# Three moves in the schedule of a two-layer graph network kernel: squares a step later, fp16 parts ahead of one-hots, key products ahead of key sums

## The chip, the cores and the metric

The kernel runs on one core of a Trainium2 chip. The metric is the device time of one execution in microseconds (us). Before the change three runs gave a median of 366.03 us (365.54 to 366.22).

## The reference

The input is `x` (1250 rows of 512 features) and 20000 edges `src -> dst`. Two layers follow one another, each on the row-normalized and rectified input:

```python
h = jnp.maximum(_layernorm(x), 0.0)
# layer 0: mean over the neighbours of the batch-normalized rows, a convolution, and attention
xn   = _batchnorm(h, norm1_g, norm1_b)
agg  = segment_sum(xn[src], dst) / maximum(deg, 1)
conv = relu(agg @ W_conv + b_conv)
qf, kf = phi(q, True), phi(k, False)            # 8 heads, exp(u - diag - max)/16 + 1e-6
kv   = einsum('bhnm,bhnd->bhmd', kf, vm)        # the key sums
attn = einsum('bhnm,bhmd->bhnd', qf, kv) * z
x = x + _batchnorm(conv + (attn @ Wo)[batch, pos] + h, norm2_g, norm2_b)
# layer 1
h = jnp.maximum(_layernorm(x), 0.0)
z = (1 + eps) * h + segment_sum(h[src], dst)
h = relu(batch_norm(relu(batch_norm(z @ W1 + b1)) @ W2 + b2))
x = x + h
```

Attention runs over 256 positions of one graph (the last of them stands for all later rows), with 8 heads of 64 and 256 random features (`proj`).

## The kernel before

The edges are never gathered. The kernel first builds the matrix `AT` of edge counts: 25 windows of 50 destinations each. For a window t, VectorE builds `S` (the one-hot lanes of the sources, `first_lanes`, L1139, one instruction of L984) and `ring` (one-hot codes, eight instructions of L988 in `first_chunks`, L1145). TensorE multiplies them into a bank (the counting of step t, eight products of 125x125 by up to 500 columns), and ScalarE copies the bank into `AT` (L779). VectorE builds the one-hots of window t+1 in its step t. The lanes of t+1 wait until the counting of t-1 is done (L1142). Behind them come the low counts of t-1 (L1236, a branch that here only gives a signal), on which later counting into the same bank waits (L1705); from step 8 all counting goes into bank 0, so the counting of step t waits for the low-counts signal of step t-1, which VectorE gives in its step t.

The rest of layer 0 is spread by hand over the 25 steps in the table `SLOTS` (L76), one entry per step and a last one. TensorE runs the pieces of its entry in their order and then the counting of the step (L1696 to L1729). ScalarE runs in each step (L753 to L793) the copies of its pieces, then the copy of `AT`, then normalization of further rows, and at the end the pieces UQ and MX. VectorE runs (L1231 to L1263) lanes, low counts, one-hots, statistics of transposed rows, and then its pieces. The pieces are:

- hT0 to hT9: transposes of the ten row tiles into `hT`. hT7 and hT9 use the same bank, so hT9 waits for ScalarE's copy of hT7.
- K, Q, V, N, PT, P: projections, norms of the heads, transposed `proj`, layout of the norms (`diag`).
- UKg and UQg, g = 0 to 3: products of the keys or queries of two heads with `proj` (the key products of a pair). UK banks 2 and 3 are released by ScalarE once the exponentials of MXg have read them.
- MXg: VectorE's row maximum `kmax` of UKg goes over TensorE to all partitions, VectorE makes `nbk` of it, and ScalarE computes `kf` with four exponentials (L636, L637) and two scalings (L642).
- KVg: TensorE sums kf times values (the key sums of a pair). It waits for both scalings of its pair.
- UQg: VectorE's `qmax` and `nbq`, ScalarE's `qf`; QTg: transposes of qf; Og: attention output.
- G0 to G9: the convolution product of row tile i. ScalarE normalizes the tile into `hn` (`normed`, L677; tile 1 in step 7, tile i+2 behind the AT copy of the step that has Gi), VectorE splits it into two fp16 parts (`normed_parts`, L1097: `hn_hi` L1102, `hn_lo` L1103), and TensorE multiplies the parts with the fp16 parts of the weights in twelve products of 128x512 columns. Tile 0 is multiplied in fp32. In VectorE's step t the parts of tile t-7 are made, t = 8 to 16. ScalarE copies the result to `hh` and VectorE makes the rest `hl` (`conv_low`, L1170), which frees the bank.
- FR: the sum of the squares of the convolution weights. ScalarE squares the weights in step `SQ_AT` (L773), TensorE sums over partitions in piece FR, GpSimd takes the inverse root (`wscale`, L513), ScalarE makes `wC_hi` behind the AT copy of the step that has FR (L780), and VectorE makes `wC_lo` in step `SPLIT_AT` = 6.
- D, A: degrees, and the aggregation over neighbours, twenty products of 400 or 450 columns each; F1, F2, TA, WO: scales of the next weights, and the output projection.

Behind step 24 the rest of the aggregation runs, then the second layer's normalization, aggregation, and two large matrix products. All engines run in the order of their program; waits are semaphores.

Of the kernel before, what the change touches and what calls it, by code (L numbers as in the profile page):

```python
# [15 lines left out]
P = 128  # L16
# [9 lines left out]
T = 10  # L26
# [34 lines left out]
for _n, _k in PARAMS:  # L61
# [12 lines left out]


SLOTS = [s.split() for s in (  # L76
# [4 lines left out]
SQ_AT, SPLIT_AT, H_AT = 2, 6, 6  # L81

SPARE = {"start": 20, "ranges": 5, "hT0": 3, "hT1": 3, "hT2": 4}

# [116 lines left out]
def gnn_kernel(nc, x, src, dst, params, eps, w_conv, wq, wk, wv, wo, proj, w1, w2, out):  # L201
    with ExitStack() as ctx:
        sems = {}

        def sem(name):
            if name not in sems:
                sems[name] = ctx.enter_context(nc.semaphore(name))
            return sems[name]
# [708 lines left out]
        def _(dve):  # L917
# [18 lines left out]
            def row_stats(i):  # L936
                dve.wait_ge(sem(f"d_x{i // 2}"), 32)
                own.step(dve.bn_stats(st_row[:, i % 2, :], x_tile(i)))  # L938
                own.step(dve.bn_aggr(mv_row[:, i, :], st_row[:, i % 2, :]))  # L939
                row_terms(i).then_inc(sem("s_mv"), 1)  # L940
# [40 lines left out]
            def lanes(slot, c):  # L981

                a = slo[:, bass.ds(c, G)].unsqueeze(1).broadcast_to([CH, P, G])
                dve.tensor_tensor(S[:, slot], iota_lane[0:CH], a, ALU.is_equal)  # L984

            def one_hot(slot, t, c, j, a, b):

                return dve.tensor_scalar(ring[:, slot, j, a:b], iota_code[0:CH, a:b], code[:, bass.ds(c + j, 1)],  # L988
                                         float(-CODES * t), ALU.subtract, ALU.is_equal)
# [70 lines left out]
            def weight_low(layer, half):  # L1060
                dve.wait_ge(sem(f"s_w{layer + 1}h"), half + 1)
                lo, hi, raw_w = ((w1_lo, w1_hi, w1_s), (w2_lo, w2_hi, w2_s))[layer]
                k = raw_w[half].shape[1]
                ks = slice(k * half, k * half + k)
                dve.scalar_tensor_tensor(lo[:, ks, :], raw_w[half][:], scale_w[layer][:, 0:1], hi[:, ks, :],
                                         ALU.mult, ALU.subtract).then_inc(sem(f"s_w{layer + 1}l"), 1)
# [25 lines left out]
            def tile_stats(i):  # L1092
                dve.wait_ge(free[PLACE[f"hT{i}"][0]], PLACE[f"hT{i}"][1] + 1)
                for f in range(FB):
                    own.mark(dve.bn_stats(st_1[:, f, i, :], hT[:, f, i * L:(i + 1) * L]))  # L1095

            def normed_parts(i):  # L1097

                dve.wait_ge(sem("s_hn"), i + 1)
                if i >= 3:  # L1100
                    dve.wait_ge(full[PLACE[f"G{i - 2}"][0]], PLACE[f"G{i - 2}"][1] + 1)
                own.step(dve.tensor_copy(hn_hi[:, i % 2], hn[:, i % 2]))  # L1102
                dve.tensor_tensor(hn_lo[:, i % 2], hn[:, i % 2], hn_hi[:, i % 2], ALU.subtract).then_inc(sem("s_hns"), 1)  # L1103
# [4 lines left out]
            def feature_terms(f, n):  # L1108
                return dve.tensor_scalar(var_eps[:, f:f + n], mv_f[:, f:f + n, 1], BN_EPS, None, ALU.add)  # L1109
# [14 lines left out]
            def low_counts(t):  # L1124

                if t == 0:
                    dve.wait_ge(sem("s_atlo0"), 1)
                with dve.If_lt(big_r, span_r):
                    dve.wait_ge(sem("s_at"), t + 1)
                    dve.tensor_tensor(at_of(ATlo, t), counts_of(t), at_of(AT, t), ALU.subtract, saturate=False)\  # L1130
                       .then_inc(sem(f"s_lo{t % 2}"), 1)
                with dve.Else():
                    dve.wait_ge(sem("s_win"), t + 1)
                    dve.sem_inc(sem(f"s_lo{t % 2}"), 1)

            def load_range(t):
                dve.load([lo_r[t % 2], out_r[t % 2]], win[t:t + 1, :])  # L1137

            def first_lanes(t):  # L1139

                if t >= 2:
                    dve.wait_ge(sem("s_win"), t - 1)  # L1142
                lanes(t % 2, dve.snap(lo_r[t % 2], min_val=0, max_val=NCH - 1))

            def first_chunks(t):  # L1145

                lo = dve.snap(lo_r[t % 2], min_val=0, max_val=NCH - 1)
                for n, j in enumerate(CHUNK_ORDER):
                    ins = one_hot(t % 2, t, lo, j, *CHUNK_COLS[j])
                    if n % Q == Q - 1:  # L1150
                        ins.then_inc(sem("s_hot"), 1)
                dve.reg_add(made, made, 1)

            def further_chunks(t):

                dve.reg_add(span_r, out_r[t % 2], 0)
                with dve.If_lt(none_r, span_r):
                    for h in range(2):
                        dve.load([from_r, to_r], ranges[2 * t + h:2 * t + h + 1, :])
                        with dve.Fori(dve.snap(from_r, min_val=0, max_val=NCH - 1),  # L1160
                                      dve.snap(to_r, min_val=1, max_val=NCH), G) as i:
                            dve.wait_ge(sem("s_grp"), dve.snap(made, min_val=1, max_val=1 << 20))
                            lanes(t % 2, i)
                            for j in range(G):
                                ins = one_hot(t % 2, t, i, j, h * HALF, (h + 1) * HALF)
                            ins.then_inc(sem("s_hotx"), 1)
                            dve.reg_add(made, made, 1)
                dve.end_ifs()
# [37 lines left out]
            def piece(name):  # L1206
                if name[0] == "A":
                    mean_rows(name)
                elif name[0] == "G":
                    conv_low(int(name[1]))  # L1210
                else:
                    attention(name)
                if name == "WO1":
                    att_in[0] = True
                    own.after(own.n)
                    for early in RAW:
                        f, ci = int(early[1]), int(early[2])
                        if early in held:
                            own.mark(feature_stats(f, ci, hT[:, f, COLS[ci][0]:sum(COLS[ci])]))
# [11 lines left out]
            for t in range(NW):  # L1231

                if t + 1 < NW:
                    first_lanes(t + 1)
                if t:
                    low_counts(t - 1)  # L1236
                further_chunks(t)
                if t + 1 < NW:
                    first_chunks(t + 1)
                if t + 2 < NW:  # L1240
                    load_range(t + 2)
                if t == 0:
                    for i in range(6, T):
                        row_stats(i)
                for name in SLOTS[t - 1] if t else ():
                    if name[:2] == "hT":
                        tile_stats(int(name[2]))
                        if name == f"hT{T - 1}":
                            own.after(own.n)
                            for f in range(FB):  # L1250
                                own.mark(dve.bn_aggr(mv_f[:, f, :], st_1[:, f].rearrange("p c s -> p (c s)")))
                            own.after(own.n)
                            feature_terms(0, FB).then_inc(sem("s_mv1"), 1)
                if t == SPLIT_AT:
                    dve.wait_ge(sem("s_wch"), 1)
                    dve.scalar_tensor_tensor(wC_lo[:], wC[:], wscale[:, 0:1], wC_hi[:], ALU.mult, ALU.subtract)\
                       .then_inc(sem("s_wcl"), 1)
                if 0 < t - H_AT - 1 < T:
                    normed_parts(t - H_AT - 1)
                for name in SLOTS[t]:  # L1260
                    piece(name)
                    if name == "O3":
                        weight_low(0, 0)  # L1263
# [612 lines left out]
```

## Time and profile before

| | |
|---|---|
| median of 3 runs | 366.03 us (365.54 to 366.22) |
| the profiled execution | 365.55 us |
| its span from first to last instruction | 363.7 us |
| TensorE busy | 348.0 us, 96% |
| VectorE busy | 246.4 us, 68% |
| ScalarE busy | 181.3 us, 50% |
| GpSimd busy | 95.2 us, 26% |
| mean granted clock of TensorE | 0.998 |

The span is the time between the first and the last instruction in the trace; the execution's time has some 1.85 us around it. All times in the rows below count from the start of the span. Busy time of TensorE is modelled: its products overlap. Steps 0 to 7 take up to about 59 us, steps 8 to 24 up to about 160 us.

### The profile page before, as it was taken

To read this page: it belongs to the slowest core of one execution; us is meant where nothing else is said; L and a number is where in the kernel's file an instruction comes from. 1 tells how busy PE (TensorE), PEld (TensorE's weight loads), DVE (VectorE), ACT (ScalarE), POOL (GpSimd) and SP (SyncE) were. 2 spreads that over 40 slices of the span, in tenths; PEclk is the share of its full clock that TensorE was granted. 3 is DMA by queue.
4 is the path that set the end of the run, shared out by engine and by line. 5 is a ranking of instruction groups with operands and counts; after the bars stand their busy time and mean duration, and the time that the engine had idled before them with its cause. 6 is when DMAs were issued, how large, how long until landed. Compare 5 with 4: busy or idle time off the path is not lost.

```text
span 363.7 us, 6194 instructions
## 1 busy us (share of the span) xinstructions
PE 348.0 (96%) x2072; PEld 224.0 (62%) x2072; DVE 246.4 (68%) x667; ACT 181.3 (50%) x302; POOL 95.2 (26%) x163
## 2 busy tenths in 40 slices
PE   7899899989999999999998999999999999999994
PEld 3678655757777666767564675455555555565562
DVE  5889999998998995867998787522464443422325
ACT  0548538768477167454437766411534645233132
POOL 8132120000000000100042778722277465101100
PEclk9999999999999999999999999999999999999999
DMA  6990303300000000034900000000000000010223
GB/s 162 289 303 30 119 1 119 118 3 1 3 3 4 3 3 3 3 97 148 264 9 3 0 2 3 2 2 1 2 0 0 2 0 2 0 51 21 70 58 85
DMA packets 13539, 18.05 MB, mean 50 GB/s; under 512 B 1839, under 2 KB 6895, under 8 KB 13491
## 3 DMA queue, kind: packets, MB, share of 16 engines
q1 hardware_dynamic: 12538, 17.21, 16.4%
q8 instruction: 26, 0.43, 0.5%
q10 hardware_dynamic: 953, 0.23, 0.3%
q14 instruction: 22, 0.18, 0.2%
HBM read 14.88 MB, written 2.56 MB: 48 GB/s over the span
## 4 chain that ended last, share of the span: by engine, by line
PE 74%; DVE 15%; issue 4%; ACT 3%; DVEq 2%; DMA 0%; POOL 0%; SPq 0%; ACTq 0%; POOLq 0%
PE bank L1424 71%; DVE ring L988 2%; DVE st L1095 2%; DVE st_row L938 2%; PE bank L1815 1%; PE bank L1454 1%; PE bank L1774 1%; ACT hn L688 1%; DVEq L1137 1%; DVE st_row L1310 1%; DVE x L1305 1%; DVE mv_row L939 1%; DVE x L1375 0%; PE bank L1635 0%; DVE ln_tmp L933 0%
## 5 line engine op out<-in xcount | busy, mean ns | idle before, releaser
L1424 PE MATMUL bank<-AT,hh 125*128 125x400 f16 (+3 forms) x250 | 81.2, 332 | 1.2 <-DVEq L1335 0.4
L1424 PE MATMUL bank<-AT,hl 125*128 125x400 f16 (+3 forms) x250 | 80.9, 332 | 0.0
L988 DVE TENSOR_SCALAR ring<-iota_code,code 125x250 f16<-125x250 f16 x200 | 46.1, 307 | 1.4 <-issue 1.4
L1424 PEld LDWEIGHTS bank<-AT,hh 125*128 125x128 f16 x250 | 24.1, 97 | 19.8 <-issue 1.1
L1424 PEld LDWEIGHTS bank<-AT,hl 125*128 125x128 f16 x250 | 24.2, 97 | 17.6 <-issue 0.2
L1424 PE MATMUL bank<-ring,S 125*128 125x250 f16 x200 | 33.5, 310 | 0.0
L1424 PE MATMUL bank<-a_hi,w_hi 128*128 128x400 f16 (+1 forms) x96 | 32.6, 340 | 0.0
L1424 PE MATMUL bank<-agg_hi,w_hi 128*128 128x400 f16 (+1 forms) x96 | 32.6, 339 | 0.0
L1424 PE MATMUL bank<-agg_hi,w_lo 128*128 128x400 f16 (+1 forms) x96 | 32.5, 339 | 0.0
L1424 PE MATMUL bank<-a_hi,w_lo 128*128 128x400 f16 (+1 forms) x96 | 32.5, 339 | 0.0
L1424 PE MATMUL bank<-agg_lo,w_hi 128*128 128x400 f16 (+1 forms) x96 | 32.5, 339 | 0.0
L1424 PE MATMUL bank<-a_lo,w_hi 128*128 128x400 f16 (+1 forms) x96 | 32.5, 338 | 0.0
L525 POOL TENSOR_SCALAR mean_w<-mean_w 128x1 f32<-128x1 f32 x2 | 0.9, 447 | 119.8 <-ACT mean_w L591 119.8
L1424 PEld LDWEIGHTS bank<-ring,S 125*128 125x128 f16 x200 | 25.7, 145 | 9.1 <-issue 1.4
L861 ACT ACTIVATE zr<-bank,par,undo_w 128x400 f32<-128x400 f32 (+1 forms) x24 | 16.0, 690 | 23.5 <-POOL a_lo L565 17.1
L565 POOL TENSOR_TENSOR a_lo<-zr,a_hi 128x1250 f16<-128x1250 f32 x7 | 22.0, 3141 | 16.7 <-DVE a_hi L1346 16.7
L1090 DVE BATCH_NORM_STATS2 st_f<-zr 128x6 f32<-128x400 f32 (+1 forms) x24 | 13.5, 588 | 18.1 <-ACT zr L861 18.1
L885 ACT ACTIVATE ur<-bank,par,undo_w 128x400 f32<-128x400 f32 (+1 forms) x12 | 8.2, 698 | 32.7 <-PE bank L1424 22.2
L500 POOL TENSOR_TENSOR bn_tmp<-var_eps,minus_half 128x1 f32<-128x1 f32 (+1 forms) x15 | 8.7, 580 | 54.5 <-DVE var_eps L1109 54.5
L591 ACT ACTIVATE AT<-bank 125x500 f16<-125x500 f32 x25 | 15.2, 606 | 12.0 <-PE bank L1424 11.9
L491 POOL TENSOR_TENSOR ln_s<-ln_tmp,minus_half 125x1 f32<-125x1 f32 x20 | 14.5, 723 | 24.3 <-DVE ln_tmp L934 24.3
L984 DVE TENSOR_TENSOR S<-iota_lane,slo 125x1024 f16<-125x1024 f16 x25 | 18.5, 742 | 2.5 <-issue 1.9
(229 smaller groups left out, 703.0 us busy)
## 6 DMA issues: line engine op xcount, KB each, us to landing
w_s<-w SPq DMA_DIRECT2D x4, 1024.0 KB, 5.2
x_in<-x SPq DMA_DIRECT2D x5, 448.0 KB
x<-x SPq DMA_DIRECT2D x2, 1120.0 KB
out<-x SPq DMA_DIRECT2D x6, 224.0 KB
wB<-wk SPq DMA_DIRECT2D x1, 1024.0 KB, 9.6
wA<-wq SPq DMA_DIRECT2D x1, 1024.0 KB, 13.8
wC<-w_conv SPq DMA_DIRECT2D x1, 1024.0 KB, 16.1
wB<-wv SPq DMA_DIRECT2D x1, 1024.0 KB, 6.3
```

The lines of the kernel that those rows point to most:

```text
L491: own.step(pool.tensor_tensor(s, ln_tmp[:, 0, i:i + n], minus_half[0:L, 0:n], ALU.pow))
L500: own.step(pool.tensor_tensor(bn_tmp[:, 1, k:k + n], var_eps[:, k:k + n], minus_half[:, 0:n], ALU.pow))
L565: pool.tensor_tensor(a_lo[:, b, :], zr[:, b % 2, :], a_hi[:, b, :], ALU.subtract)\
L591: return act.activation(o, i, ACT.Copy, scale=scale)
L861: ins = act.activation(zr[:, b % 2, c0:c0 + w], ps[:, 0:w], ACT.Identity, bias=pcol("b1", b), scale=undo_w[0][:, 0:1])
L885: ins = act.activation(ur[:, f % 2, c0:c0 + w], ps[:, 0:w], ACT.Identity, bias=pcol("b2", f), scale=undo_w[1][:, 0:1])
L938: own.step(dve.bn_stats(st_row[:, i % 2, :], x_tile(i)))
L984: dve.tensor_tensor(S[:, slot], iota_lane[0:CH], a, ALU.is_equal)
L988: return dve.tensor_scalar(ring[:, slot, j, a:b], iota_code[0:CH, a:b], code[:, bass.ds(c + j, 1)], float(-CODES * t), ALU.subtract, ALU.i ...
L1090: return dve.bn_stats(st_f[:, f, ci, :], ap)
L1095: own.mark(dve.bn_stats(st_1[:, f, i, :], hT[:, f, i * L:(i + 1) * L]))
L1424: return pe.matmul(o, l, r, start=start, stop=stop, skip_group_check=True)
```

## The change

It makes three moves. ScalarE squares the convolution weights in step 3 instead of 2 (`SQ_AT`), and FR moves from slot 4 to slot 5; with it ScalarE's `wC_hi` moves behind the AT copy of step 5. VectorE makes the fp16 parts of a row tile between the lanes and the one-hots of its step instead of behind the one-hots. In slot 13 UK2 comes before KV1 on TensorE. VectorE's and ScalarE's own order in slot 13 stays, as VectorE has no work for KV1 and ScalarE none for UK2. No instruction is added or taken away, and no DMA is moved.

```diff
-    "hT0 hT1 hT2 K0 RG K1", "hT3 hT4 PT Q0", "hT5 hT6 N1 Q1", "hT7 hT8 N0 hT9 UK0", "FR P", "UQ0 V0", "MX0 V1", "QT0",
-    "G0 UK1", "KV0 UQ1 G1", "O0 G2", "G3 MX1", "QT1 G4", "KV1 UK2 G5", "O1 UQ2 G6", "G7",
+    "hT0 hT1 hT2 K0 RG K1", "hT3 hT4 PT Q0", "hT5 hT6 N1 Q1", "hT7 hT8 N0 hT9 UK0", "P", "FR UQ0 V0", "MX0 V1", "QT0",
+    "G0 UK1", "KV0 UQ1 G1", "O0 G2", "G3 MX1", "QT1 G4", "UK2 KV1 G5", "O1 UQ2 G6", "G7",
...
-SQ_AT, SPLIT_AT, H_AT = 2, 6, 6
+SQ_AT, SPLIT_AT, H_AT = 3, 6, 6
...
                 further_chunks(t)
+                if 0 < t - H_AT - 1 < T:
+                    normed_parts(t - H_AT - 1)
                 if t + 1 < NW:
                     first_chunks(t + 1)
...
-                if 0 < t - H_AT - 1 < T:
-                    normed_parts(t - H_AT - 1)
                 for name in SLOTS[t]:
                     piece(name)
```

## Rows read from the trace of the kernel before

**Rows 1.** Busy time by stretch: start:end, length, engines, clock, DMA share, GB/s
```profile
88.39:189.00 100.61, 100.61 (x633) 70.55 (x634) 84.42 (x206) 53.08 (x91) 5.40 (x13) 1.00 0.17 49
...
90.42:111.40 20.98, 20.98 (x127) 15.28 (x128) 19.84 (x61) 12.41 (x29) 0.00 (x0) 1.00 0.01 2
```

**Rows 2.** TensorE's waits up to 200 us: line <- releaser: us, times, longest
```profile
PE bank L1424 <- issue: 1.6, 1, 1.6
PE bank L1454 <- ACT hT L591: 1.5, 1, 1.5
...
PE bank L1424 <- ACT kf L642: 0.4, 1, 0.4
```

**Rows 3.** The chain of waits, 40 to 100 us: start, us, what
```profile
53.48 0.70 DVE qmax L1019
...
59.07 18.25 PE bank L1424 x104
```

**Rows 4.** VectorE's waits, 29 to 60 us
```profile
DVE ring L988 <- issue: 0.6, 2, 0.4
```

**Rows 5.** ScalarE in order of time: start, us, instruction, [idle before <- releaser]
```profile
36.65 1.91 ACT L694 ACTIVATE sqr<-wC 128x2048 f32<-128x2048 f32 x1
...
54.76 0.47 ACT L653 ACTIVATE qf<-bank,nbq 128x256 f32<-128x256 f32 x1 [2.97 <-DVE nbq L1020]
...
64.44 1.65 ACT L688 ACTIVATE hn<-hT,bn_t,bn_s 128x125 f32<-128x125 f32 x4
...
85.37 0.46 ACT L636 ACTIVATE kf<-bank,nbk 128x256 f32<-128x256 f32 x1
...
90.12 1.65 ACT L688 ACTIVATE hn<-hT,bn_t,bn_s 128x125 f32<-128x125 f32 x4
...
111.44 0.47 ACT L636 ACTIVATE kf<-bank,nbk 128x256 f32<-128x256 f32 x1 [0.65 <-DVE nbk L1013]
```

**Rows 6.** VectorE in order of time, steps 8, 9, 10, 11, 12 and 15
```profile
64.12 1.84 DVE L988 TENSOR_SCALAR ring<-iota_code,code 125x250 f16<-125x250 f16 x8
66.13 0.42 DVE L1102 CAST hn_hi<-hn 128x500 f16<-128x500 f32 x1 [0.17 <-ACT hn L688]
...
69.32 0.83 DVE L984 TENSOR_TENSOR S<-iota_lane,slo 125x1024 f16<-125x1024 f16 x1 [0.26 <-DVE kmax L1004]
...
75.34 0.68 DVE L984 TENSOR_TENSOR S<-iota_lane,slo 125x1024 f16<-125x1024 f16 x1
75.94 1.84 DVE L988 TENSOR_SCALAR ring<-iota_code,code 125x250 f16<-125x250 f16 x8
77.69 0.42 DVE L1102 CAST hn_hi<-hn 128x500 f16<-128x500 f32 x1
78.14 0.68 DVE L1103 TENSOR_TENSOR hn_lo<-hn,hn_hi 128x500 f16<-128x500 f32 x1
...
84.71 0.17 DVE L1013 SCALAR_TENSOR_TENSOR nbk<-diag,kmaxall 128x4 f32<-128x4 f32 x1
...
89.81 0.69 DVE L1172 TENSOR_TENSOR hl<-bank,hh 125x512 f16<-125x512 f32 x1 [1.04 <-ACT hh L591]
...
106.67 0.69 DVE L1172 TENSOR_TENSOR hl<-bank,hh 125x512 f16<-125x512 f32 x1 [0.56 <-ACT hh L591]
```

**Rows 7.** TensorE in order of time: counting 9, G3, KV1, UK2, KV2
```profile
70.50 1.33 PE L1424 MATMUL bank<-ring,S 125*128 125x250 f16 x8
...
78.92 0.40 PE L1424 MATMUL bank<-wC_hi,hn_hi 128*125 128x512 f16 x1 [1.60 <-issue]
...
88.39 1.97 PE L1424 MATMUL bank<-vaug,kf 128*128 128x65 f32 x16 [0.43 <-ACT kf L642]
90.29 1.14 PE L1424 MATMUL bank<-projT,tqk 64*128 64x256 f32 x8
...
114.64 1.90 PE L1424 MATMUL bank<-vaug,kf 128*128 128x65 f32 x16
```

## The prediction

> **What bounds the kernel.** I read the table of stretches first. From 88.39 to 189 us TensorE is busy for 100.61 of 100.61 us [rows 1]: whatever moves the product that starts at 88.39 moves the end by as much, unless a new wait opens in that stretch. Then I read TensorE's own waits [rows 2]. Up to 88.39 three of them answer to the three edits: 1.5 us for a bank that ScalarE's copy of `hT` frees (at 38 us), 1.6 us ahead of 78.92 and 0.4 us ahead of 88.39. The chain of waits says which of them count [rows 3]: it goes through VectorE's qmax at 53.48, two steps of ScalarE, and TensorE from 59.07 on. So up to 59 us VectorE sets the pace, and what it waits for there is its own issue, 0.6 us in all, never another engine [rows 4]. From 59 us TensorE sets it, with VectorE close behind.
>
> **Edit 1: the squares of the convolution weights in step 3 instead of 2, FR in slot 5, wC_hi after the counts of step 5.** ScalarE's squares (about 2 us from 36.65 [rows 5]) no longer stand ahead of the copies of hT7, hT8 and N0, which then run at about 37.3 to 38.6, so hT9 on TensorE loses its wait of 1.5 us. The squares run at about 39 to 41, ahead of AT(3), whose reader is the counting of step 5. wC_hi (2 us, like the squares of the same 128x2048) lands near 50.3, where ScalarE idles 2.97 us up to 54.76 for the first nbq [rows 5]; VectorE's wC_lo wants it after 57. As VectorE waits for nobody before 59, TensorE only arrives earlier at the transposes QT0 and waits 1.5 us longer there; G0 still starts at 59.07. No DMA moves, SP's and ACT's DMA queues keep their order, and POOL's wscale comes before the batch scales as it did. Value taken: 0. Ends: -1.5 us (the whole wait of TensorE) and +0.5 us (a late wC_hi pushes the first qf).
>
> **Edit 2: the fp16 parts ahead of the next one-hots.** In step t VectorE now runs lanes(t+1), parts(t-7), eight one-hots(t+1), pieces. This first bites in step 8 with parts(1). Before, the one-hots ran from 64.12 and the parts began at 66.13 after a rest of 0.17 us of waiting for `hn` [rows 6]. That `hn` is ScalarE's work of 64.44 + 1.65 [rows 5], and nothing in the diff makes it earlier: it stands behind kf of MX0 and qfT of QT0. So VectorE now stands still from about 64.1 to 66.13, and the one-hots that filled this time come behind the parts. Queued behind the waiting instruction are the one-hots (75.94 to 77.69 in a set without a gap, so 1.76 us [rows 6]), hl(0) and kmax. All of VectorE from there on comes 1.76 us later: lanes(10) at 69.32 + 1.76 = 71.08.
> Two instructions of TensorE feel it. The counting of step 9 waits for the low-counts signal that VectorE gives right behind lanes(10); I put this at 0.3 us behind (it lies between 0 and the 0.7 us to the first one-hot): 71.4 instead of 70.50 [rows 7], 0.9 us of new idle. The other is G3, at 78.92. Its parts(3) stood behind lanes(11) at 75.34 and the one-hots at 75.94, and ended at 78.14 + 0.68 = 78.82 [rows 6]. Now lanes(11) start at 75.34 + 1.76 = 77.10, parts(3) 0.60 us later, and they end 1.13 us on (77.69 to 78.82), at 78.83. The lead given to the parts is eaten by the slip that the wait in step 8 made, and G3 starts at 78.93; the 0.9 us at step 9 vanishes in front of this. Value at G3: 0, with ends of -1.6 us (no slip arrives) and +0.3 us (0.1 us more of issue in each of three steps).
>
> **Edit 3 with the slip, steps 11 to 13.** VectorE works without a wait for others from lanes(11) to MX1's nbk, which ended at 84.71 + 0.17 = 84.88 and now ends at 86.64 [rows 6]. ScalarE's kf of MX1 started at 85.37 behind hn(5); it is now bound by nbk (0.04 us behind it) and starts at 86.68, 1.3 us later. KV1 waited for it and began at 88.39, 3.02 us behind the first instruction of kf [rows 5, 7]; KV1 can now begin at 86.68 + 3.02 = 89.7. In the old order UK2 would be stuck behind. Now UK2 (90.29 to 91.35 before, 1.06 us) goes first: its two banks are released when the fourth exponential of MX1 is done, near 88.3, so it runs from about 88.4 to 89.5, inside the wait. KV1 takes 1.90 us (88.39 to 90.29 [rows 7]), and G5 begins at 91.59 against 91.35: +0.24 us. The swap is worth its 1.06 us: without it this would be +1.3.
>
> **Further on: KV2.** Behind kf, ScalarE makes qfT(1), hh(4) and hn(6), all 1.3 us later. VectorE waited for hh(4) already, 1.04 us ahead of 89.81 [rows 6], and its lanes(14), first in a stretch that starts at 90.42, now start at 91.72. Parts(6) then have to wait for hn(6), 90.12 + 1.65 + 1.3 = 93.07 [rows 5], some 0.6 us behind the lanes. From lanes(14) to the nbk of MX2 VectorE took 20.98 us (90.42 to 111.40, 19.84 busy [rows 1]); 0.56 us of it was a wait for hh(7) [rows 6] that is covered when VectorE is late, and I take off 0.1 for smaller ones: 20.3 us. New nbk: 91.72 + 0.6 + 20.3 = 112.62, 1.22 us later. kf began at 111.44 right behind nbk, so KV2 was possible at 111.44 + 3.02 = 114.46 and started at 114.64: a margin of 0.18 us [rows 5, 7]. KV2 moves to 114.46 + 1.22 = 115.68: +1.04 us. Ends: +1.6 us (the whole slip of 1.76 less 0.18) and -0.6 us (VectorE at its 19.84 busy and no new wait). In slot 18 KV2 still stands ahead of UK3, so nothing fills this wait. After it TensorE was busy without a gap, so the shift stays.
>
> **Sum.** These are positions on one engine, one behind the other, and aren't added: 0 for edit 1, 0 at G3, +0.24 at G5, +1.04 at KV2 and at the end. The profiled execution took 365.55 us (span 363.7 and 1.85 around it), which gives 366.6; the median of the runs shown is 0.48 above that execution, so the median comes to 366.03 + 1.04 = 367.1.
>
> **A rule that speaks against this.** TensorE, the busiest engine, has gaps of 1.6 and 0.4 us on the chain and one of 1.5 off it, and the three edits meet them one by one. The Trainium skill (Perfetto Trace Analysis, Optimization Strategy) says to find the gaps of the engine that one optimizes and to make the dependencies behind them start sooner or end faster. By that rule the time falls by 2.0 us, to 364.0. That these gaps end with VectorE's parts and ScalarE's kf the trace confirms; what the rule leaves out is what the earlier start takes from the engine behind.
>
> **Rivals.**
> A, faster: the gaps close. It is one mechanism, the wait for hn(1) in step 8. If it costs VectorE less than about 0.9 us, or lanes(11) have made up for it, parts(3) end before 78.0 and G3 starts up to 1.5 us sooner. Then kf of MX1 starts at 84.92 behind the old nbk (0.45 us sooner), KV1 at 87.94 behind UK2, and G5 at 89.84: -1.5 us. From lanes(14) on VectorE's 20.3 us stand in front of KV2 again and let through 0.5 to 0.7 us of this. So 365.4, or 364.5 if they don't. For it: all three of [rows 2]. Against: an `hn` that ends at 66.1 with VectorE there at 64.1.
> B, no change that can be told: the slip arrives, but VectorE regains more than I let it (the difference between 20.3 and 19.84, and hn(6) sooner), and KV2 comes 0.2 to 0.6 us late: 366.4. For it: the margins here are tenths. Against: nothing idles on VectorE in most steps.
> C, slower by more: in each step the parts now wait for an `hn` that ScalarE makes only after the counting that also releases VectorE's lanes. If ScalarE is late with it in steps 14 to 16 too, or issue gaps of 0.2 us come in several steps, the shift at KV2 is the full 1.6 us and the counting of step 15 waits too: 367.8.
>
> **Chances and range.** My forecast 0.42, C 0.10, B 0.33, A 0.15. 0.2% (0.73 us) is about what a measurement of this kernel can tell from no change: faster by more 0.15, within it 0.33, slower by more 0.52. The range goes from A's capped case, 365.4, to just over C, 367.9; the forecast's own is 366.8 to 367.5.
>
> **What would show it.** VectorE idle for about 2 us at 64 with `hn` as releaser and its one-hots from 67.2; new idle of TensorE up to 71.4; G3 at 78.9; no wait ahead of hT9, a longer one ahead of QT0, G0 at 59.07; UK2 at 88.4 ahead of KV1 at 89.7; a wait of about 0.8 us for kf ahead of KV2. The prediction is wrong if G3 starts before 78.3 or KV2 starts without a wait.

## The result

The changed kernel takes 367.11 us (median of 8 runs, 366.97 to 367.42) against 366.02 us before (8 runs, 365.54 to 366.22): ratio 1.0029, 95% interval 1.0020 to 1.0039. It is 1.1 us slower. The profiled execution took 367.12 us, its span is 365.3 us.

TensorE's waits up to 200 us in the trace after (line <- releaser: us in total, times, longest), to be held against [rows 2]:

```profile
PE bank L1424 <- DVEq L1134: 1.7, 2, 1.2
...
PE bank L1424 <- DVE diag L999: 1.5, 1, 1.5
...
PE bank L1424 <- ACT kf L642: 0.8, 1, 0.8
PE bank L1635 <- ACT qf L654: 0.6, 1, 0.6
```

The wait for ScalarE's copy of `hT` at 38 us is gone, and so is the one of 1.6 us ahead of G3. In their place stand two waits for the low-counts signal of VectorE's sequencer (L1134, 1.7 us), one for a bank that VectorE's `diag` copy frees (1.5 us), and the wait for kf, which has grown from 0.4 to 0.8 us and moved from KV1 to KV2.

VectorE in the trace after, steps 8 to 13 and 16 (start, us, instruction, [idle before <- releaser]), to be held against [rows 6]:

```profile
63.41 0.82 DVE L984 TENSOR_TENSOR S<-iota_lane,slo 125x1024 f16<-125x1024 f16 x1
66.16 0.42 DVE L1102 CAST hn_hi<-hn 128x500 f16<-128x500 f32 x1 [1.92 <-ACT hn L688]
66.61 0.68 DVE L1103 TENSOR_TENSOR hn_lo<-hn,hn_hi 128x500 f16<-128x500 f32 x1
67.21 1.84 DVE L988 TENSOR_SCALAR ring<-iota_code,code 125x250 f16<-125x250 f16 x8
...
71.10 0.83 DVE L984 TENSOR_TENSOR S<-iota_lane,slo 125x1024 f16<-125x1024 f16 x1 [0.26 <-DVE kmax L1004]
...
77.63 0.41 DVE L1102 CAST hn_hi<-hn 128x500 f16<-128x500 f32 x1
78.07 0.68 DVE L1103 TENSOR_TENSOR hn_lo<-hn,hn_hi 128x500 f16<-128x500 f32 x1
...
86.40 0.16 DVE L1013 SCALAR_TENSOR_TENSOR nbk<-diag,kmaxall 128x4 f32<-128x4 f32 x1 [0.15 <-DVE kmaxall L1010]
...
91.06 0.69 DVE L1172 TENSOR_TENSOR hl<-bank,hh 125x512 f16<-125x512 f32 x1 [0.62 <-ACT hh L591]
...
93.06 0.42 DVE L1102 CAST hn_hi<-hn 128x500 f16<-128x500 f32 x1 [0.57 <-ACT hn L688]
...
112.39 0.16 DVE L1013 SCALAR_TENSOR_TENSOR nbk<-diag,kmaxall 128x4 f32<-128x4 f32 x1 [0.15 <-DVE kmaxall L1010]
```

The first pair of rows is where it begins: the lanes at 63.41, then 1.92 us of nothing until `hn` of tile 1 is there, and only then the parts and the one-hots. From then on VectorE is 1.7 to 1.8 us late (lanes(10) at 71.10 instead of 69.32), and it carries this to the nbk of MX1 (86.40 instead of 84.71); at the nbk of MX2 1.15 us are left (112.39 for 111.24).

ScalarE in the trace after, kf of MX1 and of MX2, to be held against [rows 5]:

```profile
86.59 0.47 ACT L636 ACTIVATE kf<-bank,nbk 128x256 f32<-128x256 f32 x1 [1.12 <-DVE nbk L1013]
...
112.58 0.47 ACT L636 ACTIVATE kf<-bank,nbk 128x256 f32<-128x256 f32 x1 [1.74 <-DVE nbk L1013]
```

TensorE in the trace after: MX0, the counting of step 9, G3, the counting of step 12, UK2, KV1, KV2, to be held against [rows 7]:

```profile
50.81 0.68 PE L1424 MATMUL bank<-ident,kmax 128*128 128x128 f32 x4 [1.45 <-DVE diag L999]
...
71.87 1.36 PE L1424 MATMUL bank<-ring,S 125*128 125x250 f16 x8 [1.18 <-DVEq L1134]
...
78.85 0.40 PE L1424 MATMUL bank<-wC_hi,hn_hi 128*125 128x512 f16 x1
...
87.31 1.36 PE L1424 MATMUL bank<-ring,S 125*128 125x250 f16 x8 [0.53 <-DVEq L1134]
88.60 1.13 PE L1424 MATMUL bank<-projT,tqk 64*128 64x256 f32 x8
89.66 2.00 PE L1424 MATMUL bank<-vaug,kf 128*128 128x65 f32 x16
...
115.63 1.97 PE L1424 MATMUL bank<-vaug,kf 128*128 128x65 f32 x16 [0.78 <-ACT kf L642]
```

G3 starts 0.07 us sooner than before, KV2 0.99 us later. As a landmark late in layer 0 I take VectorE picking up the last unit but one of the aggregation, before and after:

```profile
188.97 0.47 DVE L1192 TENSOR_TENSOR tmpr<-bank,rdb 128x300 f32<-128x300 f32 x1
```
```profile
190.03 0.47 DVE L1192 TENSOR_TENSOR tmpr<-bank,rdb 128x300 f32<-128x300 f32 x1
```

It is 1.06 us late. That agrees with the 1.09 us between the medians. The two profiled spans differ by 1.6 us, more than this. Most of the rest is one row of the chain of waits, the same instruction of GpSimd on the same data, before and after:

```profile
222.15 0.55 POOL ln_s L491
```
```profile
223.21 0.93 POOL ln_s L491
```

It took 0.38 us longer in the profiled execution after, in a place where everything waits for it. The last section shows that this step of 0.38 us comes and goes from execution to execution, in kernels of either order, so it isn't put down to the change.

### The profile page after: what moved, and what is told of

It reads as the page before. It is cut to its first block, busy times and chain, and to the rows that moved or that the text cites. A ratio compares the mean times of both kernels' runs of the same rounds, so it can differ in the third digit from the quotient of the medians.

```text
span 365.3 us, 6194 instructions
## 1 busy us (share of the span) xinstructions
PE 349.0 (96%) x2072; PEld 223.7 (61%) x2072; DVE 245.9 (67%) x667; ACT 181.6 (50%) x302; POOL 95.0 (26%) x163
## 4 chain that ended last, share of the span: by engine, by line
PE 61%; DVE 23%; issue 6%; ACT 4%; DVEq 4%; DMA 1%; POOL 0%; SPq 0%; ACTq 0%; POOLq 0%
PE bank L1424 58%; DVE ring L988 5%; DVEq L1137 2%; DVE st L1095 2%; DVE st_row L938 2%; DVE qmax L1019 1%; DVEq L988 1%; DVE kmax L1004 1%; PE bank L1815 1%; DVE hn_hi L1102 1%; PE bank L1454 1%; PE bank L1774 1%; ACT hn L688 1%; DVE S L984 1%; ACT kf L637 1%
## 5 line engine op out<-in xcount | busy, mean ns | idle before, releaser
L491 POOL TENSOR_TENSOR ln_s<-ln_tmp,minus_half 125x1 f32<-125x1 f32 x20 | 14.3, 716 | 24.8 <-DVE ln_tmp L934 24.8
```

What stands on the lines that cost most here:

```text
L491: own.step(pool.tensor_tensor(s, ln_tmp[:, 0, i:i + n], minus_half[0:L, 0:n], ALU.pow))
```

## The experiments

My theory: edit 1 is worth nothing; edit 2 makes VectorE wait for hn(1) in step 8, and this lateness takes back what the parts gained at G3 and then delays kf of MX2; edit 3 hides part of the delay at KV1. The rivals R1 to R8 stand in the expectations. Each run is compared with the kernel before on the same chip (medians 365.60 to 366.08 us).

**Edit 1 alone (e1).**

```diff
-    ... "FR P", "UQ0 V0", ...
+    ... "P", "FR UQ0 V0", ...
-SQ_AT, SPLIT_AT, H_AT = 2, 6, 6
+SQ_AT, SPLIT_AT, H_AT = 3, 6, 6
```

> Only edit 1 (squares in step 3, FR in slot 5) in the kernel before. My theory (VectorE sets the pace up to 59 us, so this edit is worth nothing; all of the loss is the wait for hn(1) that edit 2 makes in step 8): no wait ahead of hT9, about 1.5 us of new TensorE idle between 49 and 57 us, G0 at 59.1, time as before, 366.0 (+-0.2). Rival R1 (a gap that is closed on TensorE is a gain): 1.5 us less, 364.5.

Measured: 366.07 us, ratio 1.0003 (0.9994 to 1.0012). TensorE's waits show where the 1.5 us went:

```profile
PE bank L1424 <- issue: 1.6, 1, 1.6
PE bank L1424 <- DVE diag L999: 1.5, 1, 1.5
```

The wait for `hT` is gone and one of equal length for VectorE's `diag` has taken its place; that ahead of G3 is untouched. G0 stands at 59.43 for 59.07, but VectorE's first lanes, at 15.14 for 14.78, show the same 0.36 us long before the edit acts. R1 falls.

**Edit 2 alone (e2).**

```diff
                 further_chunks(t)
+                if 0 < t - H_AT - 1 < T:
+                    normed_parts(t - H_AT - 1)
...
-                if 0 < t - H_AT - 1 < T:
-                    normed_parts(t - H_AT - 1)
```

> Only edit 2 (the parts ahead of the one-hots in steps 8 to 16). My theory: VectorE idle 1.9 us ahead of parts(1), G3 at 78.9, kf of MX1 at 86.6, KV1 at 89.7 with UK2 behind it, G5 at 92.6 instead of 91.35; KV2 is reached at 115.9 and finds its kf ready (115.6), so its wait is gone: +1.27 us, 367.3. Rival R2 (the order UK2 before KV1 is what costs): as before, 366.0.

Measured: 367.99 us, ratio 1.0054 (1.0040 to 1.0068): 2.0 us slower, where I expected 1.27. R2 falls, as the loss is there without edit 3, and greater. The profile is of a longer execution (372.21 us; the other five took 367.95 to 368.05), in which TensorE's rows stand 4.31 us later already at G0 (63.38 for 59.07): KV1 at 93.89 is 89.58 on the other traces' scale. KV1, UK2 and KV2 in it:

```profile
93.89 1.97 PE L1424 MATMUL bank<-vaug,kf 128*128 128x65 f32 x16 [0.96 <-ACT kf L642]
95.79 1.13 PE L1424 MATMUL bank<-projT,tqk 64*128 64x256 f32 x8
...
120.79 1.97 PE L1424 MATMUL bank<-vaug,kf 128*128 128x65 f32 x16 [0.64 <-ACT kf L642]
```

KV1 waits 0.96 us with UK2 behind it, as expected, but KV2 waits as well, 0.64 us. VectorE says why, in steps 15 and 16:

```profile
109.72 0.42 DVE L1102 CAST hn_hi<-hn 128x500 f16<-128x500 f32 x1 [0.23 <-ACT hn L688]
...
114.18 0.42 DVE L1102 CAST hn_hi<-hn 128x500 f16<-128x500 f32 x1 [0.37 <-ACT hn L688]
```

Once TensorE is 1.2 us late (KV1 at 89.58 for 88.39), ScalarE's `hn`, made behind the counting, is late for VectorE too, and each such wait is handed on to the next nbk. This is the mechanism of my rival C. KV2, at 120.79, is 1.84 us late by the same scale, and the landmark, at 195.19, 1.91 us. So edit 3 is worth 0.85 us beside edit 2 (367.99 here to 367.14 in e10 below), not the 0.2 us that I had left for it.

**Edit 3 alone (e3).**

```diff
-    ... "KV1 UK2 G5", ...
+    ... "UK2 KV1 G5", ...
```

> Only edit 3 (UK2 ahead of KV1). My theory: UK2 runs 88.0 to 89.0 in the wait of KV1, KV1 at 89.0 without a wait, G5 0.43 us sooner, and since hh(7) and the lanes follow TensorE there, KV2 also 0.43 us sooner: 365.6. Rival R2 (the swap itself costs): 366.3 or more.

Measured: 365.92 us, ratio 0.9998 (0.9989 to 1.0007): no change, where I expected 0.43 us less. KV1 and G8 in its trace:

```profile
88.94 2.00 PE L1424 MATMUL bank<-vaug,kf 128*128 128x65 f32 x16
...
106.09 0.40 PE L1424 MATMUL bank<-wC_hi,hn_hi 128*125 128x512 f16 x1 [0.48 <-issue]
```

KV1 no longer waits, but G8 now does, for parts(8), which VectorE makes at 104.87 to 105.99 behind the one-hots of its step. G8 starts 0.11 us sooner than before (106.20), and KV2 0.13 us sooner (114.51 for 114.64). The swap doesn't cost anything (R2 falls here too); most of its gain ends at a wait that I hadn't seen. The profile names no releaser for this wait; e11 below tests it.

**Edits 1 and 3, edit 2 from step 9 on (e4).**

```diff
-                if 0 < t - H_AT - 1 < T:
+                if 1 < t - H_AT - 1 < T:
                     normed_parts(t - H_AT - 1)
...
+                if 0 < t - H_AT - 1 < 2:
+                    normed_parts(t - H_AT - 1)
                 for name in SLOTS[t]:
```

> Edits 1 and 3 as in the changed kernel, edit 2 only from step 9 on: parts(1) stay behind the one-hots of step 8, parts(2) to parts(9) come ahead of theirs. My theory: no slip is made in step 8; lanes(10) at 69.3, parts(3) end at 77.1 and G3 starts right behind the counting at 77.2, KV1 at 87.9 behind UK2, G5 at 89.8 (1.5 us sooner than before); VectorE's work from parts(6) on holds KV2 to 114.0, after a wait of about 0.85 us for kf: 0.67 us less than before, 365.35. Rival R3 (the one-hots that come later in every step hold up the counting, the one step 8 means little): 366.8 to 367.1, as the changed kernel.

Measured: 365.40 us; the ratio's interval, 0.9973 to 1.0018, holds one execution of 369.84 us, so against the kernel before it shows no change by itself; against the changed kernel the median is 1.7 us less, and it is where it was expected. G3, and KV2, in its trace:

```profile
77.21 0.38 PE L1426 MATMUL bank<-wC_hi,hn_hi 128*125 128x512 f16 x1
```
```profile
113.88 1.97 PE L1426 MATMUL bank<-vaug,kf 128*128 128x65 f32 x16 [0.78 <-ACT kf L642]
```

Eight of nine parts are still ahead of their one-hots; only step 8 is undone, and G3 starts 1.64 us sooner than in the changed kernel. R3 falls. KV2 waits for kf as expected and caps the gain.

**All three edits, hn(1) made earlier on ScalarE (e5).**

```diff
-                if t == H_AT + 1:
-                    normed(1)
                 if t < NW:
                     act.wait_ge(sem("s_win"), t + 1)
                     copy(at_of(AT, t), counts_of(t)).then_inc(sem("s_at"), 1)
+                if t == H_AT:
+                    normed(1)
```

> The changed kernel with all three edits, and hn(1) made earlier: ScalarE makes it in step 6 behind the AT copy and ahead of kf of MX0, where it idled 1.23 us, instead of in step 7. My theory (the wait for hn(1) in step 8 is the whole loss): hn(1) ends at 61.0, VectorE doesn't wait at 64, parts(3) end at 76.9, G3 right behind the counting at 77.2, KV1 at 87.8, KV2 at 113.9 after a wait of about 0.8 us: 0.7 to 0.8 us less than before, 365.25. Rival R3 (one-hots later in every step are the cost): as the changed kernel, 367.0.

Measured: 365.14 us, ratio 0.9975 (0.9965 to 0.9986): faster than before, with the changed kernel's own order of VectorE and TensorE. ScalarE's hn(1), and VectorE's parts(1), in the trace of e8, which has the same edit:

```profile
59.36 1.62 ACT L688 ACTIVATE hn<-hT,bn_t,bn_s 128x125 f32<-128x125 f32 x4
```
```profile
64.16 0.42 DVE L1102 CAST hn_hi<-hn 128x500 f16<-128x500 f32 x1
```

The parts follow the lanes at once. This takes the wait away by taking away its cause, and the loss goes with it. e5 is also ahead of e4: there VectorE still waits 0.17 us for hn(1) behind the one-hots, and its lanes(10) start at 69.36, here at 69.08; KV2 starts at 113.61 for 113.88.

**UK3 ahead of KV2, on e4 (e7) and on e5 (e8).**

```diff
-    ... "KV2 UK3 D0", ...
+    ... "UK3 KV2 D0", ...
```

> e4 (parts ahead from step 9 on) with UK3 ahead of KV2 in slot 18. My theory: the wait of 0.8 us for kf of MX2, which caps the gain of e4 at 0.6 us, is filled by UK3's 1.06 us, so the 1.5 us won at G5 reach the end: 364.5. Rival R4 (VectorE is the bound by now, another wait of TensorE takes the place): 365.3, as e4.

> e5 (hn(1) early, all parts ahead of the one-hots) with UK3 ahead of KV2. My theory: 1.6 us less than before, 364.4. Rival R4: 365.2, as e5.

Measured: e7 364.43 us, ratio 0.9953 (0.9940 to 0.9967); e8 364.18 us, ratio 0.9946 (0.9933 to 0.9960). R4 falls: with the wait for kf of MX2 filled, the 1.5 us of G5 reach the end. The counting of step 17, UK3 and KV2 in e8:

```profile
111.49 1.33 PE L1424 MATMUL bank<-ring,S 125*128 125x250 f16 x8
112.75 1.14 PE L1424 MATMUL bank<-projT,tqk 64*128 64x256 f32 x8
113.82 2.00 PE L1424 MATMUL bank<-vaug,kf 128*128 128x65 f32 x16
```

e8 is the version that beats both kernels: 1.9 us below the one before, 2.9 us below the changed one.

**UK3 ahead of KV2 in the changed kernel itself (e6).** The edit is the one of e7.

> The changed kernel with UK3 ahead of KV2 in slot 18 and nothing else. My theory (the last 0.8 us of the loss is the wait of KV2 for kf of MX2, with UK3 queued behind it): UK3 at 114.85, KV2 behind it at 115.9 without a wait, what follows 0.2 us later than before the change instead of 1.0: 366.25. Rival R8 (VectorE is late for later readers too and gives them the same delay): 367.0, as the changed kernel.

Measured: 366.11 us against 365.60 us on that chip, ratio 1.0004 (0.9988 to 1.0021). That is 0.5 us, between my 0.2 us and R8's 1.0 us, though R8's lies outside the interval. Both kernels' executions there scatter between two values 0.4 us apart (the last section shows what makes them), and most of those of e6 have the longer one, most of those before the shorter. The trace decides. UK3, KV2 and VectorE's last unit but one of the aggregation in it:

```profile
114.80 1.13 PE L1424 MATMUL bank<-projT,tqk 64*128 64x256 f32 x8
115.87 2.00 PE L1424 MATMUL bank<-vaug,kf 128*128 128x65 f32 x16
```
```profile
189.13 0.47 DVE L1192 TENSOR_TENSOR tmpr<-bank,rdb 128x300 f32<-128x300 f32 x1
```

KV2 has no wait, and the unit that stood at 188.97 before and at 190.03 in the changed kernel stands at 189.13: of the delay of 1.06 us 0.90 are gone by this swap alone. This profiled execution (365.74 us) and the one before (365.55 us) both have the shorter value, and differ by 0.19 us. R8 falls.

**e4 with VectorE late by work (e9).**

```diff
                         own.mark(dve.tensor_reduce(kmax1[:, h:h + 1], ps[:], AX.X, ALU.max))
+                        for spare in ((4, 5), (6,))[j] if name == "UK1" else ():
+                            own.mark(dve.tensor_reduce(kmax1[:, spare:spare + 1], ps[:], AX.X, ALU.max))
```

> e4 with VectorE made 1.8 us later in step 8 by work instead of a wait: three more maxima over the banks of UK1 (0.60 us each), whose results nobody reads. My theory (only VectorE's lateness from step 8 on counts, not what makes it): G3 at 78.9, KV1 at 89.7, KV2 at 115.7 after a wait, as the changed kernel: 367.1. Rival R5 (the wait or the order in step 8 itself matters, not the lateness): 365.4, as e4.

Measured: 367.17 us, ratio 1.0029 (1.0019 to 1.0040), the changed kernel's time to 0.06 us. The lanes of step 9 on VectorE, then the counting of step 9 and KV2 on TensorE:

```profile
71.15 0.83 DVE L984 TENSOR_TENSOR S<-iota_lane,slo 125x1024 f16<-125x1024 f16 x1 [0.26 <-DVE kmax L1006]
```
```profile
71.92 1.36 PE L1428 MATMUL bank<-ring,S 125*128 125x250 f16 x8 [1.21 <-DVEq L1136]
...
115.68 1.97 PE L1428 MATMUL bank<-vaug,kf 128*128 128x65 f32 x16 [0.78 <-ACT kf L642]
```

All three rows are those of the changed kernel to 0.05 us. R5 falls: it is VectorE's lateness that costs, whatever makes it.

**Edits 2 and 3 without edit 1 (e10).** The edit is that of e2 and e3 together.

> Edits 2 and 3 without edit 1. My theory (edit 1 is worth nothing in this company either): as the changed kernel, 367.1 (+-0.2), with the 1.5 us wait ahead of hT9 back and none ahead of MX0. Rival R1: later by up to 1.5 us, 368.6, if the earlier TensorE helps once the later steps are late.

Measured: 367.14 us, ratio 1.0029 (1.0017 to 1.0042). Edit 1 is worth nothing beside the others too.

**Edit 3 with parts(8) alone ahead (e11), and edits 1 and 3 with UK3 first and parts(3) alone ahead (e12).** The diff is that of e11; e12 has 10 and 3 for 15 and 8.

```diff
                 further_chunks(t)
+                if t == 15:
+                    normed_parts(8)
...
-                if 0 < t - H_AT - 1 < T:
+                if 0 < t - H_AT - 1 < T and t != 15:
                     normed_parts(t - H_AT - 1)
```

> Edit 3 and of edit 2 only parts(8), ahead of the one-hots of step 15. The run with edit 3 alone won 0.45 us at G5 and lost it again at G8 (106.09), which waited 0.48 us for parts(8). My theory (that wait alone gives the gain back): parts(8) end at 104.8, G8 at 105.7, KV2 at 114.2, 0.43 us less than before: 365.6. Rival R6 (the next wait, kf of MX2, takes its place): 366.0.

> Edits 1 and 3, UK3 ahead of KV2, and of edit 2 only parts(3), ahead of the one-hots of step 10. My theory: G3 at 77.2 and G5 1.5 us sooner as in e7, but parts(8) stay behind their one-hots on a VectorE without a pause since lanes(14), so G8 starts only 0.35 us sooner than before, at 105.75: 365.7. Rival R7 (only the gap at G3 had to be closed): 364.5, as e7.

Measured: e11 365.75 us, ratio 0.9992 (0.9983 to 1.0001), e12 365.62 us, ratio 0.9990 (0.9981 to 0.9999). In e11 G8 starts at 105.45, but a part of the gain is lost again at G9, which waits for parts(9):

```profile
110.58 0.40 PE L1426 MATMUL bank<-wC_hi,hn_hi 128*125 128x512 f16 x1 [0.33 <-issue]
```

KV2 stands at 114.36, 0.28 us sooner than before. That is between my number and R6's, and what took its place wasn't the wait that R6 names; the ratio's interval holds no change. In e12, whose profiled execution stands 0.56 us late already at G0 (59.63 for 59.07), the waits sit at G4 and G8:

```profile
84.29 0.40 PE L1426 MATMUL bank<-wC_hi,hn_hi 128*125 128x512 f16 x1 [1.22 <-issue]
...
106.25 0.40 PE L1426 MATMUL bank<-wC_hi,hn_hi 128*125 128x512 f16 x1 [0.35 <-issue]
```

The time was as expected (365.7), with one wait more than I had named. Less the 0.56 us, G3 starts at 77.17, 1.75 us sooner than before, but G4 at 83.73 only 0.30 us sooner: most of what G3 wins is lost at G4 already. G5 is 0.85 us sooner (90.50 for 91.35) and not the 1.5 us that I expected, and G8, at 105.69, is where I had it. R7 falls: the gap in front of G3 comes back at later products whose parts stand behind a set of one-hots. Moving eight of the nine (e7) brings the gain to the end; whether fewer would do was not tested.

## Why the prediction was right

- Edit 1 at 0: shown by e1 and e10. The 1.5 us wait moved as I said, but not to QT0, where the wait is 0.59 us for 0.46 before. It stands ahead of MX0 at 50.81, since MX0's bank is P's, and VectorE frees it with the `diag` copy behind its statistics. I had not followed the banks; the size is the same, as VectorE still sets the pace there.
- Edit 2's wait in step 8: 1.92 us with `hn` as releaser, lanes(10) at 71.10 (forecast 71.08). Cause shown from both sides: taken away in two ways (e4, e5) the loss goes, put back as work (e9) it returns.
- G3 at 78.85, forecast 78.93. The low-counts signal behind lanes(10) released the counting at 71.87, forecast 71.4; I had put the signal 0.3 us behind the lanes, and the start came 0.77 us behind. The error vanished ahead of G3, as the 0.9 us had to.
- The same signal made a wait of 0.53 us at the counting of step 12, of which the prediction said nothing. It was covered only just: UK2 started at 88.60, behind the counting, and ended as KV1 became possible. It is the same signal, 0.76 us behind the start of lanes(13) (86.55), so a later one would have moved KV1.
- kf of MX1 at 86.59 (86.68), UK2 at 88.60 (88.4), KV1 at 89.66 (89.7), nbk of MX2 ended at 112.55 (112.62), KV2 at 115.63 (115.68). VectorE waited for hn(6) 0.57 us (0.6) and took 91.67 to 112.55, 20.88 us, less that wait: 20.3, the value I took. G5 came at 91.50, +0.15 us for the forecast +0.24.
- The lower end at KV2, -0.6 us, doesn't follow from what stands beside it: lanes(14) at 91.72 and 19.84 us of work without a wait give an nbk at 111.56, still 0.16 us later than before, and TensorE itself is 0.24 us late. The end should have been about +0.2 us; the value that was measured, +0.99, doesn't touch it.
- The 0.48 us that the prediction put between its profiled execution and the median is about the step of GpSimd of the last section: the profile before has the short value of 0.55 us. Carrying it over was right, but nothing that the prediction shows gave a reason for it.
- What the prediction priced wrongly is edit 3. It said that without it the shift at G5 would be 1.3 us, which is about right there (1.2 us in e2, with UK2 and G5 behind KV1), but it is 2.0 us at the end, as a later TensorE makes ScalarE's `hn` late for VectorE. In the kernel as changed this second loop stays closed by 0.29 us in step 16: hn(9) ends at 108.73, parts(9) start at 109.02.
- Rival A's gain did not come in the changed kernel, as its condition, no slip in step 8, wasn't met. Where e4 and e5 met it, its cap at KV2 was right: 0.6 and 0.9 us, not 1.5, until UK3 filled the wait (e7, e8: 1.6 and 1.9 us). The Trainium skill (Perfetto Trace Analysis, Optimization Strategy) says to find what blocks the engine in its gaps and to make that start sooner or end faster. The changed kernel met all three gaps and is 1.1 us slower; e8, where the input of the parts was made sooner too and the wait at KV2 filled, gained 1.9 us of the 2.0 that the prediction worked out by that rule.
- That the end is late by KV2's wait, and not by what VectorE does after it, is shown by e6: with the wait filled the landmark at 189 us is 0.16 us late instead of 1.06, close to the +0.24 us that the prediction had at G5.

## What to carry to other kernels

Moving an instruction ahead in the order of an engine that is nearly full moves everything it may wait for ahead as well: before the move, ask when its input is ready in the first step in which the new order holds, not in the step where the gap is seen. A gap on the bounding engine that recurs with the same releaser has to be closed in all its places at once, as the next place gives the gain back. When a wait can't be removed, put independent work of the same engine in front of it, and do so for each repetition of the pattern.

## What the runs showed of the hardware that I had not expected

The same GpSimd power of a 125x1 column (`ln_s`, L491), the tenth and last of its kind on the way into the second layer, took 0.55 us in five of the fourteen profiled executions (before, e1, e5, e6, e11) and 0.93 us in the other nine; within the trace before, the ten took 0.55 to 1.11 us. Four of the five short ones were 0.37 to 0.54 us shorter than the median of their kernel's runs, and e1's 0.13 us, with 0.36 us lost at the start. So the two values 0.4 us apart in the runs fit this one instruction, which stands on the path that sets the end; what decides which value it takes isn't shown. A difference of spans between two single profiles is thus no measure of a change of 1 us here.

And a counting released by a bare signal of VectorE's sequencer (no engine work in front of it but the lanes) started 0.77 us behind the start of the lanes (71.10 to 71.87; 71.15 to 71.92 in e9; 0.76 us from 86.55 to 87.31).
